# A causal mask moved from a TensorE product into the VectorE instruction that takes the row maximum

## The chip, the cores and the metric

The kernel runs on one core of a Trainium2 chip. The metric is the device time of one execution in microseconds (us), lower is better. Three executions of the kernel before took 1413.13 to 1418.58 us, with a median of 1417.94 us.

## The reference

One layer over a batch of 2 sequences with 1024 positions and 256 features: layer norm, causal attention with 16 heads of 128, a residual, layer norm, a mixture of 32 experts (8 chosen per token, group-limited) with two shared experts, and a residual. What the change touches is the masking and the row maximum of the softmax:

```python
scores = jnp.einsum('biph,biqh->biqp', k, q)
mask = jnp.tril(jnp.ones((pos, pos), dtype=x.dtype))
masked = scores * mask - jnp.float32(10000000000.0) * (1.0 - mask)
attn = jax.nn.softmax(masked / jnp.sqrt(jnp.float32(d_head)), axis=-1)
z = jnp.einsum('biqp,biph->biqh', attn, v)
```

All inputs are float32. The kernel keeps that accuracy by splitting each operand of a product into a high and a low part and adding three products (hi·hi, lo·hi, hi·lo), in the functions `three` and its callers.

## The kernel before

**Tiles and rows.** Queries are cut into 8 blocks of 128 per sequence. For one head and one block r (0 to 7), a "row" here means the 128 queries of that block against their first `width(r)` = 128(r+1) keys. There are 2 sequences × 16 heads × 8 blocks = 256 such rows. Heads are handled two at a time (a "pair", 16 in all), so a pair has 16 rows.

**The life of a row.** TensorE computes its scores into one of two PSUM tensors `ps_s` of 1024 columns (`scores`, line 820 onwards). VectorE takes the negated row maximum `neg_max` (`maximum`, line 1310). ScalarE computes exp(score + neg_max) into `prob` and sums it with its accumulator (`exponentials`, line 1113). Once all four rows of a half (`c` = 0 or 1, 512 queries) are done, TensorE transposes `prob` block by block (`transpose`, line 841), ScalarE and VectorE split each transposed block into `pT_hi` and `pT_lo` (lines 1132 and 1327), and TensorE multiplies by v (`times_v`) and by W_O (`project_out`). A PSUM tensor is free for the row after next when that row's exponential is done.

**The mask before.** Line 827 issues, ahead of a row's scores, one bf16 product of `ident_bf` (the weights) and `causal` (128 columns), a block that is 0 on and below the diagonal and -1e30 above. It starts the accumulation in the diagonal block, and the scores of the piece that holds this block are added to it. Scores are computed in pieces of up to 512 columns and at least 256. Row 4 (640 keys) therefore takes a piece of 512 and one of 256, 128 columns more than needed.

**The order.** Each engine follows the same order, written out by hand as a string of items per pair: `R` a row's scores, maximum and exponential, `T` a transposed block, `V` its product with v, `X` a projection for a later head, `W` the product with W_O. `PAIR` serves eleven plain pairs (the first seven and the twelfth to fifteenth); `MIDDLE`, `ROUTE`, `SLOTS`, `DISPATCH` and `LAST` add the layer norms, the routing of the experts and the first of their work:

```python
T0.0 R0.0 R0.1 T0.1 T0.2 X0 R0.2 R0.3 V0.0 T0.3 X1 V0.1 V0.2 T1.0 T1.1 V0.3 X2 R1.0 R1.1 W0.0
```

Items `R0.0` to `R0.3` are rows 4 to 7 of the pair's first head. `T1.0` needs all four of their exponentials. `R2.0` to `R2.3` and `T3.0` are the same for the second head. `SLOTS` and `DISPATCH` are `PAIR` with routing steps of VectorE woven in. After the last pair come the experts, with their weights loaded from DRAM.

Of the kernel before, what the change touches and what calls it, by code (L numbers as in the profile page):

```python
# [5 lines left out]
F32 = mybir.dt.float32  # L6
# [6 lines left out]
P = 128  # L13
# [266 lines left out]
def width(r):  # L280

    return P * (r + 1)


def layer(nc, x, w_a, w_b, w_o, router, bias, experts, out):
    with ExitStack() as ctx:
        build(nc, ctx, x, w_a, w_b, w_o, router, bias, experts, out)


def build(nc, ctx, x, w_a, w_b, w_o, router, bias, experts, out):  # L290
    def sb(name, shape, dt=F32, until=ctx):
        return until.enter_context(nc.sbuf_tensor(name, shape, dt))
# [11 lines left out]
    ident, ident_bf = sb("ident", [P, P]), sb("ident_bf", [P, P], BF16)  # L304
    causal = sb("causal", [P, P], BF16)
# [27 lines left out]
    number_int = sb("number_int", [1, TILES], mybir.dt.int32)[:, :]  # L333
# [9 lines left out]
    with ExitStack() as attention:  # L343
# [4 lines left out]
        raw = [sb(f"raw{n}", [P, GU + D], F32, attention) for n in range(2)]  # L348
# [75 lines left out]
    s_scores, s_max, s_exp = sem("scores"), sem("max"), sem("exp")  # L424
# [26 lines left out]
    CONSTS = 25 + WORD  # L451
# [123 lines left out]
    def _(pool):  # L575
# [3 lines left out]
        pool.memset(ident_bf[:, :], 0.0).then_inc(s_const, 1)  # L579
        pool.memset(causal[:, :], 0.0).then_inc(s_const, 1)  # L580
        pool.wait_ge(s_const, 5)
        for m in (ident, ident_bf):
            pool.affine_select(out=m[:, :], in_=m[:, :], compare_op=ALU.not_equal, fill=1.0,
                               base=0, pattern=[[-1, P]], channel_multiplier=1).then_inc(s_const, 1)
        pool.affine_select(out=causal[:, :], in_=causal[:, :], compare_op=ALU.is_ge, fill=MASKED,
# [61 lines left out]
        pool.wait_ge(s_const, 18 + 1 + WORD)  # L647
# [128 lines left out]
    def _(pe):  # L776
        pe.sem_inc(s_pv, PV0)
        pe.wait_ge(s_const, 8)

        def three(to, w_hi, w_lo, m_hi, m_lo, start, stop, joins=False):  # L780

            pe.matmul(to, w_hi, m_hi, start=start, stop=False, skip_group_check=joins)  # L782
            pe.matmul(to, w_hi, m_lo, start=False, stop=False, skip_group_check=joins)  # L783
            return pe.matmul(to, w_lo, m_hi, start=False, stop=stop, skip_group_check=joins)  # L784
# [35 lines left out]
        def scores(a, r, row, x_need):  # L820


            pe.wait_ge(s_exp, row + EXP0 - 1)
            pe.wait_ge(s_x_free, x_need + X0)
            q = slice(r * P, (r + 1) * P)
            to = ps_s[r % 2]
            pe.matmul(to[:, r * P:(r + 1) * P], ident_bf[:, :], causal[:, :], start=True, stop=False,
                      skip_group_check=True)
            for k0 in range(0, width(r), NQ):
                k1 = max(min(width(r), k0 + NQ), k0 + 2 * P)  # L830
                diagonal = k0 <= r * P < k1
                last = three(to[:, k0:k1], q_hi[a][:, q], q_lo[a][:, q], k_hi[a][:, k0:k1],
                             k_lo[a][:, k0:k1], not diagonal, True, diagonal)
            last.then_inc(s_scores, 1)
# [252 lines left out]
    def _(act):  # L1087
# [25 lines left out]
        def exponentials(r, row):  # L1113
            act.wait_ge(s_max, row + 1)
            c, j = r // BC, r % BC
            act.activation(prob[c][:, j, 0:width(r)], ps_s[r % 2][:, 0:width(r)], ACT.Exp,  # L1116
                           bias=neg_max[:, r:r + 1],
                           accum_out=row_sum[:, c, j:j + 1]).then_inc(s_exp, 1)
# [125 lines left out]
    def _(dve):  # L1244
# [65 lines left out]
        def maximum(r, row):  # L1310
            dve.wait_ge(s_scores, row + 1)
            dve.tensor_reduce(neg_max[:, r:r + 1], ps_s[r % 2][:, 0:width(r)], AX.X, ALU.max,  # L1312
                              negate=True).then_inc(s_max, 1)
# [351 lines left out]
```

## Time and profile before

| | |
|---|---|
| median of three executions | 1417.94 us |
| the three | 1417.94, 1418.58, 1413.13 us |
| span of the profiled execution, first to last instruction | 1405.0 us |
| the median less that span | 12.9 us |
| TensorE busy | 1328.9 us (95%) |
| TensorE weight loads | 1171.3 us (83%) |
| VectorE busy | 905.6 us (64%) |
| ScalarE busy | 722.3 us (51%) |
| GpSimd busy | 571.1 us (41%) |
| mean granted TensorE clock | 0.990 of full speed |

The profiled execution has no total of its own beside the three; its span is what stands in the rows, and what lies around it (launch, and the end after the last instruction) is the 12.9 us up to the median. In the rows, a time like "154.17 0.60" means start and duration in us, PE is TensorE's product, PEld its weight load, DVE is VectorE, ACT ScalarE, POOL GpSimd. The duration of one pipelined product overlaps that of the next; the pace at which products follow each other is read from their starts.

### The profile page before, as it was taken

Reading aid. Unit: us, or ns where it says so; the run is one execution under the profiler, and the core shown is the slowest. Engines: PE = TensorE matmul, PEld = TensorE weight load, DVE = VectorE, ACT = ScalarE, POOL = GpSimd, SP = SyncE. Lnnn points to the kernel's source line nnn. Section 1 sums busy time; section 2 is a strip of 40 time slices with the busy share of each in tenths; the row PEclk is TensorE's granted clock in tenths of the full one; section 3 lists DMA queues with packets and bytes.
Section 4 is the critical chain, followed back from the end, with each engine's and each line's share of the span. In section 5 each row is a group of like instructions: output and inputs, shape, how many; then the busy total and the mean of one; then the engine's idle time right before and its main releaser. Section 6 shows DMA issues by size and latency. Waiting matters only on the chain.

```text
span 1405.0 us, 28535 instructions
## 1 busy us (share of the span) xinstructions
PE 1328.9 (95%) x8578; PEld 1171.3 (83%) x8578; DVE 905.6 (64%) x1875; ACT 722.3 (51%) x1688; POOL 571.1 (41%) x587
## 2 busy tenths in 40 slices
PE   5999999999999899999999999999889997989998
PEld 4888888888888787888778888888779887978886
DVE  5667666666667878687886666666776632345536
ACT  2655555555555555554445555555455553545443
POOL 5535535355232223213043635441003664546554
PEclk9999999999999999999999999999999998999999
DMA  3253544525533000000001201020459996899963
GB/s 118 83 173 105 188 164 133 172 97 183 164 135 102 19 20 16 16 16 20 12 31 60 66 27 68 34 86 0 151 202 311 368 337 237 307 363 378 302 200 116
DMA packets 128246, 195.98 MB, mean 139 GB/s; under 512 B 10400, under 2 KB 99744, under 8 KB 128160
## 3 DMA queue, kind: packets, MB, share of 16 engines
q1 hardware_dynamic: 64752, 110.04, 23.4%
q10 hardware_dynamic: 51120, 51.26, 10.9%
q0 software_dynamic: 12288, 33.57, 6.8%
q8 instruction: 50, 0.82, 0.2%
q14 instruction: 36, 0.29, 0.1%
HBM read 107.79 MB, written 87.03 MB: 139 GB/s over the span
## 4 chain that ended last, share of the span: by engine, by line
PE 82%; DVE 7%; issue 3%; ACT 3%; DMA 3%; another core or an unknown queue 1%; SPq 1%; ACTq 0%; POOL 0%; POOLq 0%; DVEq 0%
PE ps_s L782 9%; PE ps_t L841 8%; PE ps_s L784 8%; PE ps_s L783 8%; PE ps_x L782 6%; PE ps_x L783 6%; PE ps_x L784 6%; PE ps_z L782 5%; PE ps_z L784 5%; PE ps_z L783 5%; PE ps_t L1006 3%; PE ps_z L1006 3%; PE ps_s L975 2%; PE ps_t L782 2%; PE ps_t L783 2%
## 5 line engine op out<-in xcount | busy, mean ns | idle before, releaser
L1116 ACT ACTIVATE prob<-ps_s,neg_max 128x128 f32<-128x128 f32 (+7 forms) x256 | 189.4, 741 | 256.3 <-DVE neg_max L1312 252.1
L1327 DVE TENSOR_TENSOR pT_lo<-ps_t,pT_hi 128x512 fp32r<-128x512 f32 (+2 forms) x320 | 189.4, 603 | 104.9 <-ACT pT_hi L1132 101.3
L1132 ACT ACTIVATE pT_hi<-ps_t 128x512 fp32r<-128x512 f32 (+2 forms) x320 | 161.4, 533 | 94.8 <-PE ps_t L841 92.1
L1312 DVE TENSOR_REDUCE neg_max<-ps_s 128x1 f32<-128x128 f32 (+7 forms) x256 | 186.8, 748 | 14.0 <-PE ps_s L784 11.5
L679 POOL DMA_INDIRECT xs<-xn,slots x128 | 127.7, 997 | 134.8 <-PE ps_z L1006 67.6
L841 PE MATMUL ps_t<-ident,prob 128*128 128x128 f32 x1152 | 170.8, 274 | 9.4 <-ACT prob L1116 4.2
L841 PEld LDWEIGHTS ps_t<-ident,prob 128*128 128x128 f32 x1152 | 136.7, 140 | 33.1 <-DVE pT_lo L1327 5.7
L782 PE MATMUL ps_s<-k_hi,q_hi 128*128 128x512 f32 (+2 forms) x384 | 154.7, 403 | 0.0
L1524 DVE TENSOR_TENSOR h<-sg,ps_s 128x256 f32<-128x256 f32 x112 | 46.9, 418 | 155.9 <-ACT sg L1166 103.9
L782 PE MATMUL ps_s<-ring,a_hi 128*128 x384 | 125.5, 327 | 14.3 <-SPq L530 11.9
L784 PE MATMUL ps_s<-k_hi,q_lo 128*128 128x512 f32 (+2 forms) x384 | 133.7, 348 | 0.0
L783 PE MATMUL ps_s<-k_lo,q_hi 128*128 128x512 f32 (+2 forms) x384 | 132.7, 346 | 0.0
L594 POOL TENSOR_TENSOR a_hi<-raw_a,zero 128x512 fp32r<-128x512 f32 x32 | 33.3, 1041 | 243.3 <-PE ps_x L784 158.3
L782 PE MATMUL ps_z<-pT_hi,v_hi 128*128 128x512 f32 (+2 forms) x320 | 121.8, 381 | 0.5 <-DVE pT_lo L1327 0.5
L784 PE MATMUL ps_z<-pT_hi,v_lo 128*128 128x512 f32 (+2 forms) x320 | 115.5, 361 | 0.0
L783 PE MATMUL ps_z<-pT_lo,v_hi 128*128 128x512 f32 (+2 forms) x320 | 115.4, 361 | 0.0
L1166 ACT ACTIVATE sg<-ps_s 128x256 f32<-128x256 f32 x112 | 43.5, 388 | 139.3 <-PE ps_s L784 82.2
L783 PE MATMUL ps_s<-ring,a_hi 128*128 x384 | 109.9, 286 | 0.1
L784 PE MATMUL ps_s<-ring,a_lo 128*128 x384 | 109.5, 285 | 0.0
L1342 DVE SCALAR_TENSOR_TENSOR acc<-ps_t,inv_sum,acc 128x256 f32<-128x256 f32 x256 | 108.2, 474 | 0.2 <-PE ps_t L784 0.2
L782 PEld LDWEIGHTS ps_s<-ring,a_hi 128*128 128x128 f32 x384 | 74.3, 194 | 24.3 <-issue 22.0
L594 POOL TENSOR_TENSOR o_hi<-raw_o,zero 128x256 fp32r<-128x256 f32 x32 | 20.7, 647 | 168.1 <-PE ps_z L784 167.8
(306 smaller groups left out, 3682.9 us busy)
## 6 DMA issues: line engine op xcount, KB each, us to landing
ring<-ws SPq DMA_DIRECT2D x56, 512.0 KB
xs<-taken SPq DMA_DIRECT2D x16, 1536.0 KB, 9.8
xq<-xs ACTq DMA_DIRECT2D x48, 512.0 KB
xs<-yq ACTq DMA_DIRECT2D x48, 512.0 KB
ws<-split_to SPq DMA_DIRECT2D x34, 512.0 KB, 3.1
raw<-experts_dram SPq DMA_DIRECT2D x34, 256.0 KB, 3.4
raw_a<-w_a_dram SPq DMA_DIRECT2D x15, 512.0 KB, 4.4
ring_down<-experts_dram SPq DMA_DIRECT2D x56, 128.0 KB
```

Of the source, the lines that this page charges most:

```text
L594: pool.tensor_tensor(hi, src, zero[:, 0:1].to_broadcast([P, src.shape[-1]]), ALU.add).then_inc(s_pool, 1)
L679: pool.indirect_dma_start(xs[b], bass.IndirectOffsetOnAxis(ap=slots[b][:, t, k:k + 1], axis=0), xn[:, t, :], None).then_inc(s_xs[b], 16)
L782: pe.matmul(to, w_hi, m_hi, start=start, stop=False, skip_group_check=joins)
L783: pe.matmul(to, w_hi, m_lo, start=False, stop=False, skip_group_check=joins)
L784: return pe.matmul(to, w_lo, m_hi, start=False, stop=stop, skip_group_check=joins)
L841: last = pe.transpose(bank[:, j * P:(j + 1) * P], prob[c][:, j, n * P:(n + 1) * P], ident[:, :])
L1006: last = pe.matmul(to, hT[g % 2][:, at], downs[g][j], start=what == "m" or j == 0, stop=what == "m" or j == 1)
L1116: act.activation(prob[c][:, j, 0:width(r)], ps_s[r % 2][:, 0:width(r)], ACT.Exp, bias=neg_max[:, r:r + 1], accum_out=row_sum[:, c, j:j + 1 ...
L1132: act.activation(to, ps_t[m % 2][:, j * P:], ACT.Copy).then_inc(s_hi, 1)
L1312: dve.tensor_reduce(neg_max[:, r:r + 1], ps_s[r % 2][:, 0:width(r)], AX.X, ALU.max, negate=True).then_inc(s_max, 1)
L1327: dve.tensor_tensor(lo, ps_t[m % 2][:, j * P:], hi.bitcast(F32), ALU.subtract).then_inc(s_bank_free, 1)
L1342: last = dve.scalar_tensor_tensor(to, ps_t[m % 2][:, j * D:(j + 1) * D], inv_sum[:, c, q:q + 1], to, ALU.mult, ALU.add)
```

## The change

The mask product and its identity go. `causal` becomes 128×1024, zero except for its last 128 columns, which hold the triangle, so that its last `width(r)` columns are the whole mask of row r. VectorE adds them in the instruction that takes the maximum. That instruction writes -(score + mask) back into PSUM and leaves the minimum of it in `neg_max`; ScalarE's exponential reads the negated scores with a scale of -1. Row 4 is put into columns 128 to 767 of its PSUM tensor and computed in pieces of 384 and 256 columns. A semaphore increment (`s_row`, for which nobody waits) stands between VectorE's wait and the new instruction. To make room, `raw[1]` shrinks to the part that is used, and `number_int` shares memory with `score`.

```diff
+def row_of(bank, r):
+    first = P if r == 4 else 0
+    return bank[:, first:first + max(width(r), 2 * P)]
...
-    ident, ident_bf = sb("ident", [P, P]), sb("ident_bf", [P, P], BF16)
-    causal = sb("causal", [P, P], BF16)
+    ident = sb("ident", [P, P])
+    causal = sb("causal", [P, S], BF16)
...
-    number_int = sb("number_int", [1, TILES], mybir.dt.int32)[:, :]
+    number_int = flat(score)[0:1, 0:TILES].bitcast(mybir.dt.int32)
...
-        raw = [sb(f"raw{n}", [P, GU + D], F32, attention) for n in range(2)]
+        raw = [sb(f"raw{n}", [P, GU + (D, 32)[n]], F32, attention) for n in range(2)]
...
-        pool.memset(ident_bf[:, :], 0.0).then_inc(s_const, 1)
         pool.memset(causal[:, :], 0.0).then_inc(s_const, 1)
-        pool.wait_ge(s_const, 5)
-        for m in (ident, ident_bf):
-            pool.affine_select(out=m[:, :], in_=m[:, :], compare_op=ALU.not_equal, fill=1.0,
-                               base=0, pattern=[[-1, P]], channel_multiplier=1).then_inc(s_const, 1)
-        pool.affine_select(out=causal[:, :], in_=causal[:, :], compare_op=ALU.is_ge, fill=MASKED,
+        pool.wait_ge(s_const, 4)
+        pool.affine_select(out=ident[:, :], in_=ident[:, :], compare_op=ALU.not_equal, fill=1.0,
+                           base=0, pattern=[[-1, P]], channel_multiplier=1).then_inc(s_const, 1)
+        pool.affine_select(out=causal[:, S - P:], in_=causal[:, S - P:], compare_op=ALU.is_ge, fill=MASKED,
                            base=0, pattern=[[-1, P]], channel_multiplier=1).then_inc(s_const, 1)
...
             q = slice(r * P, (r + 1) * P)
-            to = ps_s[r % 2]
-            pe.matmul(to[:, r * P:(r + 1) * P], ident_bf[:, :], causal[:, :], start=True, stop=False,
-                      skip_group_check=True)
-            for k0 in range(0, width(r), NQ):
-                k1 = max(min(width(r), k0 + NQ), k0 + 2 * P)
-                diagonal = k0 <= r * P < k1
+            to, k0 = row_of(ps_s[r % 2], r), 0
+            for k1 in [NQ - P, width(r)] if r == 4 else [NQ, width(r)] if r > 3 else [max(width(r), 2 * P)]:
                 last = three(to[:, k0:k1], q_hi[a][:, q], q_lo[a][:, q], k_hi[a][:, k0:k1],
-                             k_lo[a][:, k0:k1], not diagonal, True, diagonal)
+                             k_lo[a][:, k0:k1], True, True)
+                k0 = k1
             last.then_inc(s_scores, 1)
...
-            act.activation(prob[c][:, j, 0:width(r)], ps_s[r % 2][:, 0:width(r)], ACT.Exp,
-                           bias=neg_max[:, r:r + 1],
+            act.activation(prob[c][:, j, 0:width(r)], row_of(ps_s[r % 2], r)[:, 0:width(r)], ACT.Exp,
+                           bias=neg_max[:, r:r + 1], scale=-1.0,
                            accum_out=row_sum[:, c, j:j + 1]).then_inc(s_exp, 1)
...
             dve.wait_ge(s_scores, row + 1)
-            dve.tensor_reduce(neg_max[:, r:r + 1], ps_s[r % 2][:, 0:width(r)], AX.X, ALU.max,
-                              negate=True).then_inc(s_max, 1)
+            dve.sem_inc(s_row, 1)
+            row = row_of(ps_s[r % 2], r)[:, 0:width(r)]
+            dve.tensor_tensor_reduce(out=row, in0=row, in1=causal[:, S - width(r):], scale=-1.0,
+                                     scalar=-NEVER, op0=ALU.add, op1=ALU.min,
+                                     accum_out=neg_max[:, r:r + 1]).then_inc(s_max, 1)
```

The string that orders the items is the same; what changes is what an item issues. On TensorE, the start of a plain pair (`T0.0`, then the scores of rows 4 and 5) stood like this before; the rows name line, operation, output and inputs, and columns:

```order
L841 MATMUL ps_t<-ident,prob 128x128 x4
L823 REGISTER_ALU
L824 ISA
L827 MATMUL ps_s<-causal,ident_bf 128x128
L782 MATMUL ps_s<-k_hi,q_hi 128x512
L783 MATMUL ps_s<-k_lo,q_hi 128x512
L784 MATMUL ps_s<-k_hi,q_lo 128x512
L782 MATMUL ps_s<-k_hi,q_hi 128x256
L783 MATMUL ps_s<-k_lo,q_hi 128x256
L784 MATMUL ps_s<-k_hi,q_lo 128x256
L827 MATMUL ps_s<-causal,ident_bf 128x128
L782 MATMUL ps_s<-k_hi,q_hi 128x512
```

The same place in the changed kernel, where the lines of the three products are 787 to 789:

```order
L843 MATMUL ps_t<-ident,prob 128x128 x4
L828 REGISTER_ALU
L829 ISA
L787 MATMUL ps_s<-k_hi,q_hi 128x384
L788 MATMUL ps_s<-k_lo,q_hi 128x384
L789 MATMUL ps_s<-k_hi,q_lo 128x384
L787 MATMUL ps_s<-k_hi,q_hi 128x256
L788 MATMUL ps_s<-k_lo,q_hi 128x256
L789 MATMUL ps_s<-k_hi,q_lo 128x256
L787 MATMUL ps_s<-k_hi,q_hi 128x512
```

Both mask products are gone and row 4's first piece has 384 columns; nothing else moved. On VectorE, the same stretch before (`T0.0`'s low part, the reciprocal, the maxima of rows 4 and 5, and the next low part):

```order
L1327 TENSOR_TENSOR pT_lo<-ps_t,pT_hi 128x512
L1331 RECIPROCAL inv_sum<-row_sum 128x4
L1311 ISA
L1312 TENSOR_REDUCE neg_max<-ps_s 128x1
L1311 REGISTER_ALU
L1312 TENSOR_REDUCE neg_max<-ps_s 128x1
L1326 REGISTER_ALU
L1327 TENSOR_TENSOR pT_lo<-ps_t,pT_hi 128x384
```

and in the changed kernel:

```order
L1332 TENSOR_TENSOR pT_lo<-ps_t,pT_hi 128x512
L1336 RECIPROCAL inv_sum<-row_sum 128x4
L1313 ISA
L1316 ISA ps_s,neg_max<-ps_s,causal 128x640
L1316 ISA neg_max 128x1
L1313 REGISTER_ALU
L1316 ISA ps_s,neg_max<-ps_s,causal 128x768
L1316 ISA neg_max 128x1
L1331 REGISTER_ALU
L1332 TENSOR_TENSOR pT_lo<-ps_t,pT_hi 128x384
```

Each maximum has become two instructions: one that passes over the row, and one that only writes `neg_max`, 128x1.

## Rows read from the trace of the kernel before

**Rows 1.** The page: busy time of each engine, share of the span, instructions.

```profile
PE 1328.9 (95%) x8578; PEld 1171.3 (83%) x8578; DVE 905.6 (64%) x1875; ACT 722.3 (51%) x1688; POOL 571.1 (41%) x587
```

**Rows 2.** Stretches: start:end and length in us, then busy (instructions) of PE, PEld, DVE, ACT, POOL, granted clock, DMA share, GB/s.

```profile
156.25:215.21 58.96, 58.96 (x378) 51.95 (x377) 39.54 (x78) 32.55 (x76) 27.66 (x24) 1.00 0.46 151
...
650.69:718.57 67.88, 61.95 (x380) 52.34 (x379) 58.55 (x114) 32.51 (x78) 16.38 (x14) 1.00 0.05 16
sum 267.09, PE 251.69 PEld 215.78 DVE 213.33 ACT 135.51 POOL 64.76; mean PE 62.92 PEld 53.95 DVE 53.33 ACT 33.88 POOL 16.19
```

**Rows 3.** Order of time on PE in the third pair, from `T0.0` on.

```profile
154.17 0.60 PE L841 MATMUL ps_t<-ident,prob 128*128 128x128 f32 x4
154.61 0.22 PE L827 MATMUL ps_s<-causal,ident_bf 128*128 128x128 bf16 x1
...
154.95 0.39 PE L783 MATMUL ps_s<-k_lo,q_hi 128*128 128x512 f32 x1
155.18 0.40 PE L784 MATMUL ps_s<-k_hi,q_lo 128*128 128x512 f32 x1
...
155.77 0.23 PE L827 MATMUL ps_s<-causal,ident_bf 128*128 128x128 bf16 x1
...
156.12 0.39 PE L783 MATMUL ps_s<-k_lo,q_hi 128*128 128x512 f32 x1
...
156.94 0.71 PE L841 MATMUL ps_t<-ident,prob 128*128 128x128 f32 x5
157.40 0.47 PE L782 MATMUL ps_x<-xT_hi,b_hi 128*128 128x512 f32 x1
157.71 0.39 PE L783 MATMUL ps_x<-xT_lo,b_hi 128*128 128x512 f32 x1
...
159.88 0.34 PE L783 MATMUL ps_s<-k_lo,q_hi 128*128 128x384 f32 x1
160.05 0.34 PE L784 MATMUL ps_s<-k_hi,q_lo 128*128 128x384 f32 x1
```

**Rows 4.** Groups by shape on DVE: count, busy us, mean ns, idle before.

```profile
L1312 DVE TENSOR_REDUCE neg_max<-ps_s 128x1 f32<-128x1024 f32 x32 | 39.1, 1221 | 4.9 <-PE ps_s L784 4.9
L1312 DVE TENSOR_REDUCE neg_max<-ps_s 128x1 f32<-128x896 f32 x32 | 34.6, 1080 | 0.4 <-PE ps_s L784 0.4
...
L1477 DVE TENSOR_TENSOR room<-room,best 128x1024 f32<-128x1024 f32 x2 | 2.4, 1215 | 0.0
```

**Rows 5.** The same view, one source more and one operation more: 256 columns from PSUM.

```profile
L1342 DVE SCALAR_TENSOR_TENSOR acc<-ps_t,inv_sum,acc 128x256 f32<-128x256 f32 x256 | 108.2, 474 | 0.2 <-PE ps_t L784 0.2
...
L1327 DVE TENSOR_TENSOR pT_lo<-ps_t,pT_hi 128x256 fp32r<-128x256 f32 x64 | 26.8, 418 | 16.0 <-ACT pT_hi L1132 14.7
```

**Rows 6.** Order of time on DVE in the same pair.

```profile
156.16 0.17 DVE L1331 RECIPROCAL inv_sum<-row_sum 128x4 f32<-128x4 f32 x1
156.25 1.85 DVE L1312 TENSOR_REDUCE neg_max<-ps_s 128x1 f32<-128x640 f32 x2
...
160.94 2.22 DVE L1312 TENSOR_REDUCE neg_max<-ps_s 128x1 f32<-128x896 f32 x2
```

**Rows 7.** Order of time on ACT and PEld: row 7's exponential and `T1.0`.

```profile
163.20 1.12 ACT L1116 ACTIVATE prob<-ps_s,neg_max 128x1024 f32<-128x1024 f32 x1
164.21 0.19 ACT L1116 ACTIVATION_READ_ACCUMULATOR prob<-ps_s,neg_max 128x1 f32 x1
...
164.72 0.57 PEld L841 LDWEIGHTS ps_t<-ident,prob 128*128 128x128 f32 x5
```

**Rows 8.** The second head of the same pair, ACT and PE: row 7, `T3.0`.

```profile
192.91 0.19 ACT L1116 ACTIVATION_READ_ACCUMULATOR prob<-ps_s,neg_max 128x1 f32 x1
...
194.23 1.03 PE L841 MATMUL ps_t<-ident,prob 128*128 128x128 f32 x8
```

**Rows 9.** Stretch around a fall of the granted clock (columns as in rows 2).

```profile
478.00:484.00 6.00, 4.20 (x21) 3.67 (x22) 5.00 (x9) 2.88 (x6) 2.87 (x3) 0.61 0.22 70
```

**Rows 10.** Order of time on POOL at the start, its first wait.

```profile
8.68 1.05 POOL L603 TENSOR_TENSOR inv<-var,neg_half 128x4 f32<-128x4 f32 x1 [6.29 <-DVE var L1263]
```

More of the change, by code:

```diff
@@ L423, in build @@
     s_pool = sem("pool_hi")
-    s_scores, s_max, s_exp = sem("scores"), sem("max"), sem("exp")
+    s_scores, s_row, s_max, s_exp = sem("scores"), sem("row"), sem("max"), sem("exp")
     s_bank, s_hi, s_bank_free = sem("bank"), sem("pT_hi"), sem("bank_free")
@@ L450, in build @@
     WS0, YS0 = 16, 16
-    CONSTS = 25 + WORD
+    CONSTS = 23 + WORD
     X_SCORES = [X0 + x_before + count_of(order, ("M", b, 0)) + 1
@@ L646, in _ @@
         pool.iota(thr_int, pattern=[[P, NT]], base=0, channel_multiplier=0).then_inc(s_const, 1)
-        pool.wait_ge(s_const, 18 + 1 + WORD)
+        pool.wait_ge(s_const, 16 + 1 + WORD)
         pool.tensor_copy(number[:, :], number_int).then_inc(s_const, 1)
@@ L777, in _, with three @@
         pe.sem_inc(s_pv, PV0)
[L778 to L784, printed above, removed]
+        pe.wait_ge(s_const, 6)
+        def three(to, w_hi, w_lo, m_hi, m_lo, start, stop):
+            pe.matmul(to, w_hi, m_hi, start=start, stop=False)
+            pe.matmul(to, w_hi, m_lo, start=False, stop=False)
+            return pe.matmul(to, w_lo, m_hi, start=False, stop=stop)
         def transpose_xn(q, d, bank):
```

## The prediction

> **What bounds the kernel now.** I read the page's busy times first [rows 1]: TensorE is busy for 95% of the span, VectorE for 64%, ScalarE for 51%. The average hides stages, so the second view was the stretch of one pair from row 4 to the next pair's row 4 [rows 2]. In a plain pair TensorE is busy for all of its 58.96 us, VectorE for 39.5, ScalarE for 32.6: TensorE sets the pace, and whatever leaves its queue is time won as long as the other engines keep up. In the four pairs with layer norm and routing in them (`MIDDLE` to `DISPATCH`, together 267.1 us) TensorE is busy for 251.7 us and VectorE for 213.3, and in the last of them for 61.95 and 58.55 of 67.88 us: there TensorE waits for VectorE in places. The third view is the order of time [rows 3, 6, 7], which tells what a mask product costs and how close the other engines are behind.
>
> **Removed: 256 mask products.** A product's cost is its part of the pace. Before row 5, the mask starts at 155.77 and the second score product at 156.12, 0.35 us for the mask and the first score product [rows 3]. The next 512-column product takes 0.23 (154.95 to 155.18). So the mask costs 0.12 us: a few hundredths of its own, and the rest in the product behind it, whose weights had no long product to load under. Behind transposes one could think that the following product is late anyway. Four transposes, mask and first product take 0.78 us (154.17 to 154.95), five transposes and a first product without a mask 0.77 (156.94 to 157.71), so one transpose (about 0.11) pays for the mask there too, and 0.12 us stands. 256 × 0.12 = **30.7 us**.
>
> **Removed: 128 columns of row 4.** Three products of 512 + 256 columns become three of 384 + 256. A product of 512 takes 0.23 us, one of 384 takes 0.17 to 0.18 (159.88 to 160.05), so 3 × 0.055 = 0.165 us per row 4, of which there are 32: **5.3 us**. TensorE's part is 36.0 us, and of a plain pair 16 × 0.12 + 2 × 0.165 = 2.25 us.
>
> **Changed: 256 maxima on VectorE.** The pass over the row is one source and one output more. For 1024 columns the reduction from PSUM takes 1221 ns and a two-source addition in SBUF, written in place, 1215 [rows 4], so another stream costs nothing that these rows show. None shows VectorE writing PSUM. New beyond doubt is the second instruction that only writes `neg_max`, and the increment of `s_row`. Lower bound for the addition per row: 0 (it hides, or the pass is as much shorter). Upper bound: ScalarE's instruction of the same kind takes 0.19 us [rows 7], and an operation more costs 474 - 418 = 56 ns in the pair of rows nearest to it [rows 5], together 0.25 us. The nearest row to a tiny VectorE instruction is the reciprocal of 128x4: it starts at 156.16 and the next at 156.25 [rows 6], 0.09 us. I take **0.12 us**, this and 0.03 for the increment and a longer start; 0 and 0.25 go to the range.
>
> **What covers this, and where the cover ends.** VectorE has 19 us free in a plain pair and 16 × 0.12 = 1.9 us more is no load. The delay counts where TensorE waits for an exponential. The tightest place is `T1.0`: row 7's sum is out at 164.21 + 0.19 = 164.40 and the weight load of `T1.0` starts at 164.72, a margin of 0.32 us [rows 7]. The path to it is one chain through all four maxima of the head (rows 4 and 5 back to back from 156.25, rows 6 and 7 from 160.94 [rows 6], their exponentials, and low parts between), which starts behind the projection ahead of `T0.0`. Between `T0.0` and `T1.0` TensorE itself loses four masks and one row 4, 0.645 us, so it would come 0.33 us before row 7 is ready, even if the maxima cost what they did; four maxima at 0.12 add 0.48. `T1.0` then waits for 0.81 us. A plain pair keeps 2.25 - 0.81 = 1.44 us. The second head's place is wider: its sum is out at 193.10 and `T3.0` starts at 194.23 [rows 8], 1.13 us against 0.645 + 0.48, just enough. Eleven plain pairs: **15.8 us**.
>
> In the four full pairs, in which TensorE is idle for 15.4 us already [rows 2], I take the margin of 0.32 us as used up, and of the twelve other maxima I count half on the path, 0.72 us: 2.25 - 0.81 - 0.32 - 0.72 = 0.4 us, four times: **2 us** rounded. `LAST` has 12 rows, two of them row 4: 1.77 - 0.81 = **1 us**. The first four rows, ahead of the pairs: **0.5 us**.
>
> **Costed at nothing.** GpSimd's longer memset of `causal` (its time at the start is covered by a wait of 6.29 us [rows 10]; if it were not, less than 1 us), the shared memory, the smaller `raw[1]`, and ScalarE's scale. The experts come behind and move as a block; their waits for weight loads start from the end of attention.
>
> **Sum.** 15.8 + 2 + 1 + 0.5 = 19.3 us. Span 1405.0 - 19.3 = 1385.7; the 12.9 us around it up to the median give 1398.6, say **1399 us**, 1.3% under the median of 1417.94.
>
> **Rivals.**
> *A. The maxima cost no more, and little is given back.* For it: the equal rows of 1221 and 1215 ns. Against it: two instructions stand where one did. At 0 us per row a plain pair keeps 2.25 - 0.33 = 1.92, eleven keep 21, the full four 1.6 each, the rest 2.5: 30 us, 1388. Chance 0.15.
> *B. The maxima cost 0.25 us.* `T1.0` waits 0.33 + 1.0, a plain pair keeps 0.92, eleven keep 10. In the full pairs 2.25 - 1.33 - 0.32 - 1.5 = -0.9 each, `LAST` and the first rows give 0.9: 8 us, 1410. Chance 0.17, and 0.08 beside it that the full pairs lose more still, so that nothing is seen (1411 to 1425).
> *C. Slower: the pass runs at half pace, because it reads and writes the same PSUM bank.* No row here has VectorE write PSUM, so nothing excludes it. 128 columns cost 1221 - 1080 = 141 ns [rows 4]. Rows 4 to 7 have 26 such blocks, 3.7 us more in the chain to `T1.0`, which then waits 4.5 us. The chain to `T3.0` gets the same, and with its margin and idle stretches I count 1.9. A plain pair would lose 4.5 + 1.9 - 2.25 = 4.15, eleven 46; the full pairs would get 10 us of VectorE work on top of 53 and lose 8 each: 32. That is 1496 us. It decides from a mean of (2.25 - 0.33) / 4 = 0.48 us more per maximum of rows 4 to 7, where a plain pair gains nothing. Chance 0.09.
> [...]
> *D. Slower through the clock.* [...] Against it: the pair from 650.69 has 5.9 us of idle TensorE in it and a clock of 1.00 [rows 2]. Chance 0.03.
>
> **The numbers.** The forecast has 0.48, A 0.15, B 0.25 with its tail, C and D 0.12. Faster by over 0.5% (under 1410.8; about 0.5% is what a measurement of this kernel can tell from no change): the forecast, A, and most of B's 0.17, 0.77. Within 0.5%: 0.11. Slower: 0.12. The range runs from 1386, just under A, to 1414, just over B; outside it are C, D and part of B's tail.
>
> **What would show it.** No mask products: 8322 products on TensorE instead of 8578, as the pieces keep their number. The start-to-start pace of a plain pair 57.5 us instead of 58.96, with TensorE waiting for the exponential at `T1.0` by about 0.8 us and nowhere else. The new pass at 1.22 us for 1024 columns, the instruction behind it at 0.09 us of pace. Wrong would be: a pass of over 2 us for 1024 columns (C), waits of the full pairs over 5 us more than before (B's tail), a lower clock within the pairs (D), or no wait at `T1.0` (A).

## The result and the profile after

| | before | after |
|---|---|---|
| median, us | 1416.13 (4 executions, 1413.13 to 1418.58) | 1396.44 (4 executions, 1393.97 to 1397.29) |
| ratio after / before, 95% interval | | 0.9866, 0.9846 to 0.9886 |
| span of the profiled execution | 1405.0 | 1394.4 |

The change makes the kernel 1.3% faster, as forecast (1399 us). The page of the changed kernel, busy times of the engines, against [rows 1]:

```profile
PE 1302.5 (93%) x8322; PEld 1155.3 (83%) x8322; DVE 915.7 (66%) x2131; ACT 720.8 (52%) x1688; POOL 571.7 (41%) x585
```

TensorE has 256 products and 26.4 us of work less, VectorE 256 instructions and 10.1 us more. The same stretches as in [rows 2], from a pair's row 4 to the next pair's: a plain pair, then the last of the four full ones.

```profile
153.04:210.47 57.43, 57.23 (x362) 50.91 (x361) 40.12 (x94) 32.55 (x76) 27.66 (x24) 1.00 0.46 156
...
637.69:705.86 68.17, 59.98 (x364) 51.19 (x363) 59.11 (x131) 32.64 (x78) 16.82 (x15) 1.00 0.05 16
```

The plain pair went from 58.96 to 57.43 us. TensorE is now idle for 0.2 us in it, which it never was before. The full pair, 67.88 before, is 0.3 us longer: VectorE is busy for 59.11 us of it, 58.55 before, and TensorE is idle for 8.2 us instead of 5.9; its waits for an exponential grew from 1.7 to 2.9 us.

**VectorE's new instructions**, groups by shape in the columns of [rows 4]:

```profile
L1316 DVE CUSTOM_DVE_ANT_0 ps_s<-ps_s,causal 128x1024 f32<-128x1024 f32 x32 | 40.1, 1252 | 0.0
L1316 DVE DVE_READ_ACCUMULATOR2_ANT neg_max<- 128x1 f32 x256 | 36.1, 141 | 0.0
L1316 DVE CUSTOM_DVE_ANT_0 ps_s<-ps_s,causal 128x896 f32<-128x896 f32 x32 | 34.9, 1091 | 0.2 <-PE ps_s L789 0.2
```

A pass that reads PSUM and `causal` and writes PSUM takes 1252 ns for 1024 columns where the reduction took 1221, and 1091 for 896 where it took 1080. The second source, the second operation and the writing back into PSUM together cost 31 and 11 ns. So with one source in PSUM, the other the bf16 `causal`, and the output in PSUM, the pass isn't at half pace: rival C needed over 2 us for 1024 columns.

In order of time on DVE, the chain to `T1.0` in the third pair (start, duration), beside [rows 6]:

```profile
153.04 0.81 DVE L1316 CUSTOM_DVE_ANT_0 ps_s<-ps_s,causal 128x640 f32<-128x640 f32 x1
153.76 0.14 DVE L1316 DVE_READ_ACCUMULATOR2_ANT neg_max<- 128x1 f32 x1
153.76 1.00 DVE L1316 CUSTOM_DVE_ANT_0 ps_s<-ps_s,causal 128x768 f32<-128x768 f32 x1
...
158.67 1.26 DVE L1316 CUSTOM_DVE_ANT_0 ps_s<-ps_s,causal 128x1024 f32<-128x1024 f32 x1
159.85 0.14 DVE L1316 DVE_READ_ACCUMULATOR2_ANT neg_max<- 128x1 f32 x1
```

The instruction that writes `neg_max` and the next pass start at the same moment, 153.76. It costs VectorE no pace here; but ScalarE can only start when it is over (159.85 + 0.14 = 159.99, and the exponential stands at 160.02 below).

And its end on ACT, then on PE, beside [rows 7]:

```profile
160.02 1.11 ACT L1118 ACTIVATE prob<-ps_s,neg_max 128x1024 f32<-128x1024 f32 x1
161.04 0.19 ACT L1118 ACTIVATION_READ_ACCUMULATOR prob<-ps_s,neg_max 128x1 f32 x1
```

```profile
160.69 0.28 PE L788 MATMUL ps_z<-pT_lo,v_hi 128*128 128x256 f32 x1
160.81 0.28 PE L789 MATMUL ps_z<-pT_hi,v_lo 128*128 128x256 f32 x1
161.28 1.15 PE L843 MATMUL ps_t<-ident,prob 128*128 128x128 f32 x8 [0.20 <-ACT prob L1118]
162.19 0.36 PE L787 MATMUL ps_z<-pL_hi,v_hi 128*128 128x256 f32 x1
```

Row 7's sum is out at 161.23 and `T1.0` starts at 161.28: a margin of 0.05 where it was 0.42 to the product and 0.32 to its weight load. The products before it go at 0.12 us, so `T1.0` would have started at 160.93 and waits for 0.35 us. This is the wait that the prediction named, at less than half of its length. The second head's margin shrank from 1.13 to 0.90 us and decides nothing.

### The profile page after: what moved, and what is told of

Its sections match the earlier page's. It is cut to its first block, busy times and chain, and to the rows that moved or that the text cites. A ratio compares the mean times of both kernels' runs of the same rounds, so it can differ in the third digit from the quotient of the medians.

```text
span 1394.4 us, 28532 instructions
## 1 busy us (share of the span) xinstructions
PE 1302.5 (93%) x8322; PEld 1155.3 (83%) x8322; DVE 915.7 (66%) x2131; ACT 720.8 (52%) x1688; POOL 571.7 (41%) x585
## 4 chain that ended last, share of the span: by engine, by line
PE 67%; DVE 12%; issue 9%; ACT 5%; DMA 3%; another core or an unknown queue 2%; SPq 1%; ACTq 1%; DVEq 0%; POOL 0%; POOLq 0%
PE ps_t L843 7%; PE ps_s L787 6%; PE ps_s L789 6%; PE ps_s L788 6%; PE ps_x L787 5%; PE ps_x L788 5%; PE ps_x L789 5%; PE ps_z L787 4%; PE ps_z L789 4%; PE ps_z L788 4%; DVE ps_s L1316 4%; DMA ring_down<-experts_dram 3%; PE ps_z L1008 3%; PE ps_t L1008 3%
## 5 line engine op out<-in xcount | busy, mean ns | idle before, releaser
L1316 DVE CUSTOM_DVE_ANT_0 ps_s<-ps_s,causal 128x128 f32<-128x128 f32 (+7 forms) x256 | 190.3, 769 | 5.7 <-remote 3.5
L843 PE MATMUL ps_t<-ident,prob 128*128 128x128 f32 x1152 | 172.2, 275 | 17.0 <-ACT prob L1118 10.6
L787 PE MATMUL ps_s<-k_hi,q_hi 128*128 128x512 f32 (+2 forms) x384 | 141.3, 368 | 1.2 <-DVE k_lo L1309 1.1
```

What stands on the lines that cost most here:

```text
L787: pe.matmul(to, w_hi, m_hi, start=start, stop=False)
L843: last = pe.transpose(bank[:, j * P:(j + 1) * P], prob[c][:, j, n * P:(n + 1) * P], ident[:, :])
L1316: dve.tensor_tensor_reduce(out=row, in0=row, in1=causal[:, S - width(r):], scale=-1.0, scalar=-NEVER, op0=ALU.add, op1=ALU.min, accum_out= ...
```

## The experiments

The runs stood on four chips of one kind, here A to D, and each ratio is to the kernel before on the same chip: 1408.7 us on A, 1414.6 on B, 1377.0 on C and 1414.8 on D. A pair's time is always from its row 4 to the next pair's, from the profiled execution.

### Row 4 alone, masks kept (A)

```diff
-            for k0 in range(0, width(r), NQ):
-                k1 = max(min(width(r), k0 + NQ), k0 + 2 * P)
+            for k1 in [NQ - P, width(r)] if r == 4 else ...
```

> The kernel before with one part of the change alone: row 4 in columns 128 to 767, in pieces of 384 and 256. Theory (TensorE pays for every column and there is margin at T1.0): 3 x 0.055 = 0.165 us per row 4, a plain pair of the first seven 58.63 us instead of 58.96, 4 to 5 us in all. Rival (the first-row weights or a wait eat it, so that the pieces give nothing): 58.96 us and no difference.

Measured: 1403.84 us (9 executions), ratio 0.9974 (0.9957 to 0.9991). A plain pair takes 58.63, 0.33 less, as worked out in the prediction. Item by item of TensorE's order (start to start), `R0.0` got 0.153 and `R2.0` 0.162 us shorter, and no other item moved by more than 0.02.

### Masks left out, nothing else (A)

```diff
-            pe.matmul(to[:, r * P:(r + 1) * P], ident_bf[:, :], causal[:, :], start=True, stop=False,
-                      skip_group_check=True)
```

This kernel leaves the causal mask out of the computation.

> The kernel before without the mask products and without any mask; the causal mask is left out of the computation, maxima as before, pieces of 512 and 256. Theory: 16 x 0.12 us less of TensorE per pair, of which T1.0 gives back 0.48 - 0.32 = 0.16, so 57.2 us per plain pair of the first seven. If pairs 12 to 15 were paced by something other than TensorE's queue, as in the changed kernel, they stay at 59.8 us and the whole is 16 to 19 us faster; if that was due to VectorE's new instructions, they fall to 58.0 and the whole is 24 us faster.

Measured: 1384.68 us (4), ratio 0.9827 (0.9803 to 0.9851), 24 us faster. Pairs 12 to 14 take 57.80, 57.83 and 57.82 us, which is the number of the branch that blamed VectorE's new instructions. The cause it named can't be right, as the kernel before has 59.8 us there without them; the scatters below give another, and the 24 us aren't the price of the masks alone.

A plain pair takes 57.41, almost what it takes in the changed kernel, though row 4 still has its 768 columns. The expected 57.2 had a wait at `T1.0` in it. There is none: the margin is 0.14 us. The chain from the start of row 4's pass to row 7's sum takes 7.95 us here and 8.15 before, because row 5's scores come earlier too. Before, row 5's pass waited for them and started 0.89 us behind row 4's (156.25 in [rows 6]):

```profile
157.14 0.96 DVE L1312 TENSOR_REDUCE neg_max<-ps_s 128x1 f32<-128x768 f32 x1
```

Here it starts 0.71 us behind, right after row 4's, and in the changed kernel 0.72 (153.04 and 153.76 above). In a plain pair of the changed kernel, then, the 0.33 us of row 4 and what the passes on VectorE cost cancel.

Item by item the masks are worth 0.10 to 0.14 us in each of the 16 rows, behind transposes too, 1.83 in sum. Of it 0.27 comes back where no mask stood: `T1.1`, `V0.3` and `X2` (0.17), `V3.6` (0.09). These are hand-overs of their own. In the second to sixth pair, `T1.1` starts 0.06 to 0.08 us behind the end of VectorE's `pL_lo`, which frees its PSUM tensor, where it was 0.36 before; `X2` 0.05 behind `k_lo`, which frees `ps_x`, where it was 0.27; and `V3.6` 0.05 behind `pT_lo`, its input, where it was 0.15 to 0.17. TensorE comes so early there that it meets the other engine's work, with no wait long enough to stand in the list of waits.

### The changed kernel with a product of the mask's shape put back (A)

```diff
             to, k0 = row_of(ps_s[r % 2], r), 0
+            pe.matmul(to[:, r * P:(r + 1) * P], causal[:, S - P:], causal[:, 0:P], start=True, stop=True)
```

> The changed kernel with a product of the mask's shape put back in front of each row (128 columns, bf16, own weights), whose result the scores overwrite. Theory: TensorE's queue is back but for row 4, and VectorE's new instructions are covered: a plain pair of the first seven 58.65 us, the whole 4 us faster than before and 15 us slower than the changed kernel. Rival (a good part of the gain came from VectorE or from elsewhere, such as the chip that ran it): the whole stays near the changed kernel's time. Rival (the new instructions cost on their own, more than 0.1 us per row): 59.3 us or more and slower than before.

Measured: 1410.87 us (10), ratio 1.0015 (1.0002 to 1.0028). The whole gain is gone, so it came from the products. The sizes were missed: the whole was expected 4 us faster than before and is 2 us slower, and a plain pair takes 58.87, not 58.65. Against the kernel with row 4 alone VectorE's new form costs 7.0 us. In the two profiles 1.5 us of that lie in the first seven plain pairs and 3.0 in the four full pairs (268.36 and 265.37 us), 1.8 of them in the first, which varies by 1.0 us between executions of the changed kernel; the rest lies in pairs 12 to 15, whose pace varies too. In a plain pair it is 0.24 us more than with row 4 alone. That kernel differs by VectorE's passes and by what its extra product reads and how the scores join it. The items say where:

| item | row 4 alone | product put back | |
|---|---|---|---|
| `T1.0` | 0.437 | 0.479 | +0.042 |
| `T1.1` | 0.356 | 0.412 | +0.056 |
| `V0.3` | 0.437 | 0.471 | +0.034 |
| `X2` | 1.390 | 1.505 | +0.115 |

No other item differs by over 0.02. TensorE doesn't wait for anything here (its pace into `T1.0` is 0.118 us, the margin 0.07), and still the four items from `T1.0` on take 0.25 us more. With a margin of 0.42 they don't. Here too `T1.1` starts 0.05 us behind `pL_lo` (0.36 with row 4 alone) and `X2` 0.05 behind `k_lo` (0.26). Both of these values are made behind row 7's exponential and come later with it.

The chain from row 4's pass to row 7's sum is 0.34 us longer than in the other kernel, 8.33 against 8.00: here VectorE's new form costs **0.085 us per maximum**. About 0.1 us of the 0.34 belong to this kernel: row 5's pass, whose scores have only just arrived, starts 0.89 us behind row 4's, where the reduction started 0.74 behind. In the changed kernel the pass starts 0.72 behind, and its chain of 8.19 us against the 7.95 without masks, where no pass waits for scores either, gives **0.06 us per maximum**. The passes of 640 to 1024 columns are 0.01 to 0.04 us longer than the reductions, 0.023 in the mean. The rest is the write of `neg_max`, which delays ScalarE by 0.06 to 0.07 us behind rows 5 and 7; the increment of `s_row` is in it and wasn't priced alone.

### Row 4 back to 512 + 256 in the changed kernel (B)

```diff
-            for k1 in [NQ - P, width(r)] if r == 4 else ...
+            for k1 in [NQ, NQ + 2 * P] if r == 4 else ...
```

`row_of` starts row 4 at column 0 again.

> The changed kernel with row 4 in pieces of 512 and 256 as before. Theory (what TensorE saves ahead of T1.0 is taken by the wait there, the second head's row 4 stays won): 57.43 + 0.17 = 57.6 us per plain pair. If T1.0's wait took nothing of it: 57.76 us. If it took all: 57.43 us. Whole kernel 2 to 3 us slower than the changed one.

Measured: 1398.02 us (4), ratio 0.9896 (0.9872 to 0.9919), 2.9 us above the changed kernel on the same chip. A plain pair takes 57.66, 0.23 more. `R0.0` and `R2.0` lose 0.175 each, and `V0.2`, the item in which TensorE waits for `T1.0`, gets 0.110 shorter. Row 4's narrower piece in the first head is thus worth only a third of its size; the second head's is kept in full.

### The scatters of the experts' rows left out (A)

The changed kernel's plain pairs take 57.43 us, but the stretches of pairs 12 to 14, by the same string, took 59.84, 59.80 and 59.79, and before the change 59.87, 59.75 and 59.76. What these pairs have beside the others are GpSimd's scatters, 16 per pair. This kernel leaves the 64 scatters out, so the experts of the first sequence compute on zeros:

```diff
                 pool.wait_ge(s_pv, PV0 + p * TRS + v)
-                scatter(0, (p - PAIRS - 3) * 16 + done + n)
+                pool.sem_inc(s_xs[0], 16)
```

> The changed kernel, with GpSimd's 64 scatters of the first sequence's tokens in pairs 12 to 15 left out (a semaphore increment stands for each, so the experts of the first sequence compute on zeros). Theory (GpSimd's bursts of indirect DMAs hold back TensorE's semaphore increments by about 1.5 us, so that T2.0 waits and pairs 12 to 15 keep 59.8 us): those pairs fall to 57.4 us, 8 to 9 us in all. Rival (the pace comes from the code of those pairs, their loop or their instruction loads, not from the DMAs): 59.8 us as before.

Measured: 1384.62 us (4), ratio 0.9832 (0.9812 to 0.9853). Pairs 12 to 14 take 57.44, 57.49 and 57.42: plain pairs again. Pair 15 takes 56.56, and the four together 228.91 us, 7.7 to 8.5 less than in three executions of the changed kernel with the scatters; 8 to 9 were expected. What the scatters do is seen in two places of pair 12 of the changed kernel (chip D). The first, on DVE, then on PE:

```profile
729.23 0.28 DVE L1332 TENSOR_TENSOR pL_lo<-ps_t,pL_hi 128x128 fp32r<-128x128 f32 x1
731.15 0.70 DVE L1316 CUSTOM_DVE_ANT_0 ps_s<-ps_s,causal 128x512 f32<-128x512 f32 x1 [1.64 <-remote]
```

```profile
728.76 0.39 PE L789 MATMUL ps_s<-k_hi,q_lo 128*128 128x512 f32 x1
...
732.77 0.98 PE L843 MATMUL ps_t<-ident,prob 128*128 128x128 f32 x7 [1.00 <-ACT prob L1118]
```

The last product of `R1.3` ends at 729.15, but VectorE, idle since 729.51, gets to its row only at 731.15, 2.0 us behind. In plain pairs the lag is 0.27. Row 3's exponential is late by that much, and TensorE stands at `T2.0` for 1.0 us: the 1.7 us of extra lag less the margin of 0.64 that `T2.0` has in plain pairs. The second place is the projection `X8`, on ACT, then on PE:

```profile
748.72 0.38 ACT L1106 ACTIVATE v_raw<-ps_x 128x256 f32<-128x256 f32 x1 [2.17 <-remote]
```

```profile
746.79 0.28 PE L789 MATMUL ps_x<-a_hi,xT_lo 128*128 128x256 f32 x1
...
749.89 0.39 PE L787 MATMUL ps_x<-a_hi,xT_hi 128*128 128x256 f32 x1 [0.96 <-DVE v_lo L1300]
```

`X8`'s last product ends at 747.07 and ScalarE gets to it at 748.72, 1.65 us behind; in plain pairs the lag is 0.04. VectorE's `v_lo` is late with it, and TensorE stands at `X9` for 1.0 us. Start to start, the two places take 1.2 us each of the 2.4 by which the pair is longer than a plain one. Without the scatters both lags are gone (0.27 and 0.04 us).

### The changed kernel again (B)

> The changed kernel unaltered, for a comparison on the chip of the other experiments. Plain pairs 57.43 us, pairs 12 to 14 59.8 us; ratio to the kernel before 0.987 as on the first chip, so 1390 us where the kernel before takes 1408.

Measured: 1395.1 us (4), ratio 0.9874 (0.985 to 0.9898). Plain pairs 57.43, pairs 12 to 14 59.81, 59.85 and 58.75. In the third, `R1.3`'s pass starts 23.18 us behind row 4's, as in plain pairs, and 24.9 in the two others. Of the 1.3 us by which the third is longer than plain, 1.1 stand at `X9`, as ScalarE starts 1.52 us behind `X8`.

### Scatters placed otherwise (B)

The changed kernel issues 3, 8 and 5 scatters per pair, at three places of GpSimd's order. These kernels issue 3, 2 and 11, and 3, 4 and 9. The diff is that of the first; the second has `(5, 7, 9, 11)` and `range(14, 23), 7`.

```diff
-                paced_scatters(p, range(5, 13), 3)
+                paced_scatters(p, range(5, 7), 3)
...
-                paced_scatters(p, range(14, 19), 11)
+                paced_scatters(p, range(14, 25), 5)
```

> The changed kernel with GpSimd's scatters of pairs 12 to 15 at other places: 3, 2 and 11 per pair instead of 3, 8 and 5, so that none runs in the microseconds ahead of the scores of row 3 of the second head (R1.3). Theory (a burst of indirect DMAs holds back TensorE's increments, and R1.3 is where this hurts): pairs 12 to 14 fall to about 57.5 us, 6 to 7 us in all. Rival (the late burst holds back other increments with less slack, the transposes of T3): 58.5 us or more, little gained.

> The same scatters, 3, 4 and 9 per pair, each behind another product with v, so that few stand back to back. Theory that it takes a burst: 57.5 to 58 us in pairs 12 to 14. Rival (each single scatter holds increments back): 59 us or more.

Measured: 1400.07 us, ratio 0.9901 (0.9877 to 0.9924), and 1398.47 us, ratio 0.9884 (0.9865 to 0.9903). `R1.3`'s lag is gone in both (its pass starts 23.2 us behind row 4's as in plain pairs), and pairs 12 to 14 still take 59.7 and 59.5. The wait for `v_lo` stays (3.7 and 3.6 us in 4 waits; 2.9 in 4 in the changed kernel on this chip), and one for `z_lo` is new (2.6 and 2.5 us in 4), behind an exchange whose lag was 0.3 us before and is 1.4 us here. So the delay went with the scatters that were moved, and the one at `X8` remained. Both expected gains stayed out, and neither kernel beats the changed one.

### V0.3 ahead of T1.0, and X2 ahead of T1.0 (C)

Two attempts to put work under the wait at `T1.0`, by the string of the plain pair alone:

```diff
-... V0.2 T1.0 T1.1 V0.3 X2 R1.0 ...
+... V0.2 V0.3 T1.0 T1.1 X2 R1.0 ...
```

```diff
-... V0.2 T1.0 T1.1 V0.3 X2 R1.0 ...
+... V0.2 X2 T1.0 T1.1 V0.3 R1.0 ...
```

> The changed kernel with one item of the plain pair moved on all engines: V0.3 stands ahead of T1.0 instead of behind T1.1. If the wait of TensorE at T1.0 (0.35 us, and a slower restart of about 0.1) is what eats the gain of row 4 there, V0.3's three products (about 0.36 us) lie under it: a plain pair takes 57.0 to 57.1 instead of 57.43, 13 pairs by this string give 4 to 5 us, the kernel takes about 1391. Rival: the wait is only moved, to the scores of row 0 of the other half or to X2, and the pair stays at 57.43, the kernel at 1396. Slower: the split of T0.3 isn't ready so early and V0.3 waits for it.

> The changed kernel with X2 ahead of T1.0 instead of behind V0.3. X2 is over 1 us of products, more than T1.0's wait, so TensorE would not wait there at all: a plain pair 57.0 if nothing else is late. Rival: T1.0 and T1.1 come later by what is left of X2 and the low parts that follow them make V1.0 or R1.0 wait, or X2 itself waits for its bank, since X1 stands closer before it: a plain pair of 57.4 or more, the kernel at 1396 or above.

Measured: 1362.12 us (4), ratio 0.9892 (0.9877 to 0.9907), and 1398.73 us (5), ratio 1.0154 (1.014 to 1.0167). Both fail: a plain pair takes 57.75 and 60.24. PE in the first, then PE in the second, each at its new wait:

```profile
161.85 0.28 PE L789 MATMUL ps_z<-pT_hi,v_lo 128*128 128x256 f32 x1
162.82 0.39 PE L787 MATMUL ps_z<-pL_hi,v_hi 128*128 128x256 f32 x1 [0.68 <-DVE pL_lo L1332]
163.04 0.28 PE L788 MATMUL ps_z<-pL_lo,v_hi 128*128 128x256 f32 x1
```

```profile
169.29 0.50 PE L787 MATMUL ps_x<-xT_hi,b_hi 128*128 128x512 f32 x1 [1.58 <-DVE k_lo L1309]
```

`V0.3` needs `pL_lo`, whose high part ScalarE makes only behind row 7's exponential (161.13 in the changed kernel), later than `T1.0` could start. `X2`, right behind `V0.2`, finds X1 still in `ps_x`: it waits 1.58 us for VectorE's `k_lo` (161.92 in the changed kernel), which stands behind row 7's pass and ScalarE's `k_hi`. Neither leaves room under the wait. The changed kernel itself didn't run on C, so the ratios can't be set against its own; the pace of a plain pair, 57.43 in three executions on other chips, can.

In one point both runs differ from those of the changed kernel on B: pairs 12 to 14 take 57.79, 57.74 and 57.79 in the first and 60.25, 60.23 and 60.25 in the second, each kernel's plain pace, with all their scatters in them. `R1.3`'s row there, DVE then PE:

```profile
730.21 0.69 DVE L1316 CUSTOM_DVE_ANT_0 ps_s<-ps_s,causal 128x512 f32<-128x512 f32 x1
```

```profile
729.54 0.40 PE L789 MATMUL ps_s<-k_hi,q_lo 128*128 128x512 f32 x1
```

The product ends at 729.94 and the pass starts 0.27 us behind it, though GpSimd issues a scatter every 1.27 us here as well. At `X8` the lag is 0.04 us.

### Both kernels on one chip (D)

> The kernel before, once more, for a profile on the same chip as the changed kernel's. In the runs so far with the scatters in them pairs 12 to 14 took 59.5 to 60.7 us, but in the two last runs (V0.3 first, X2 first), on a chip where the kernel before took 1377 us, they took what the plain pairs take. If the late increments are a property of the chip and not of the kernel, then where the kernel before has a median of about 1377, its pairs 12 to 14 take 58.96 like the plain ones and what follows the last pair about 423 us; where it has about 1416, they take 59.8 and 448.

> The changed kernel once more, on the same chip as the run before it. Plain pairs 57.43 on any chip. If the chip is one where the kernel before takes about 1377, pairs 12 to 14 take 57.4 too, attention gains 11 x 1.52 + 1.9 + 1 = 20 us or a little more between the spans, and the ratio comes near 0.985. If it is one of about 1416, pairs 12 to 14 stay at 59.8 and the ratio at 0.987 has to come from somewhere behind the pairs.

Measured: the kernel before 1415.07 us (12 executions), ratio 0.9997 (0.9983 to 1.0011); the changed kernel 1396.27 us (5), ratio 0.9884 (0.9865 to 0.9903). The profiled execution of the kernel before took 1415.76 us around a span of 1414.0. Its stretches (columns as in [rows 2]), the four full pairs, pairs 12 to 14, pair 15, and what follows:

```profile
451.88:719.03 267.15, 251.71 (x1559) 215.81 (x1558) 213.36 (x460) 135.57 (x317) 64.76 (x70) 0.99 0.06 17
719.03:901.19 182.16, 178.32 (x1130) 156.14 (x1129) 118.87 (x230) 96.69 (x228) 86.54 (x84) 1.00 0.16 52
901.19:961.08 59.89, 58.74 (x373) 51.34 (x372) 38.95 (x76) 31.76 (x75) 27.58 (x27) 1.00 0.17 59
961.08:1414.00 452.92, 405.62 (x2770) 365.12 (x2768) 237.00 (x529) 217.78 (x509) 195.67 (x198) 0.98 0.74 254
```

The same stretches of the changed kernel, in an execution of 1396.27 us around a span of 1394.5:

```profile
441.77:706.24 264.47, 244.08 (x1495) 211.24 (x1495) 215.39 (x525) 135.17 (x317) 65.16 (x71) 0.99 0.06 17
706.24:884.94 178.70, 173.34 (x1082) 153.08 (x1081) 120.72 (x278) 96.72 (x228) 86.35 (x83) 1.00 0.16 53
884.94:942.99 58.05, 56.97 (x358) 50.29 (x357) 39.59 (x92) 31.80 (x75) 27.57 (x27) 1.00 0.18 61
942.99:1394.50 451.51, 404.68 (x2758) 363.56 (x2755) 237.33 (x542) 217.76 (x509) 197.00 (x198) 0.98 0.74 255
```

| stretch | forecast gain | gain, us |
|---|---|---|
| up to the first pair's row 4 | 0.5 | -0.43 |
| first seven plain pairs | 7 x 1.44 = 10.1 | 10.56 (413.11 to 402.55) |
| four full pairs | 2 | 2.68 |
| pairs 12 to 14 | 4.3 | 3.46 |
| pair 15 | 1.4 | 1.84 |
| last pair and experts | 1 | 1.41 |
| sum of the span | 19.3 | 19.5 |

The first and last rows are no gain or loss of the change. The first row 4 starts at 37.6 to 39.4 us in all these profiles, in no order. The last pair itself, from its row 4 to its last product with W_O, takes 53.22 us before and 53.31 after, and the experts behind it take 394.8 to 399.7 us in five executions of these two kernels.

In this execution of the kernel before pairs 12 to 14 took 60.9, 60.7 and 60.6 us, 1 us more each than in the profile ahead of the prediction, and 59.8 was expected on such a chip. The extra us is the wait at `X9`: ScalarE gets to `X8` 1.6 us behind it here and 0.8 us in the first profile, where the 0.78 us of margin in a plain pair just covered that. The changed kernel's first profile had the 1.6 us, and a wait at `T2.0` longer by 0.5 us, so between the two first profiles these pairs kept nothing. The pair of executions whose spans, 1405.0 and 1394.4, differ by 10.6 us misled: the first was a quick one, in these pairs and in the experts (448 us against 453). The changed kernel's pairs 12 to 14 take 59.86, 59.93 and 58.91 us here, about the expected 59.8, but its gain doesn't come from behind the pairs, as was expected with that: nearly all of it lies in them.

## Why the prediction was right, point by point

**Removed: the mask products, 0.12 us each, 30.7 us.** Right as a price in the plain pairs. Their items in a plain pair sum to 1.83 us in the kernel without masks and to 1.90 in the changed one, against 16 x 0.12 = 1.92. That transposes ahead of them hide nothing is right too.

**Removed: 128 columns of row 4, 0.165 us each.** Right: 0.153 and 0.162 where it was done alone.

**Changed: the maxima, 0.12 us each.** Right in kind, too large: 0.06 us on the chain of the changed kernel, 0.085 where a pass waits for its scores. The reasoning about the small instruction took its pace from the reciprocal [rows 6], 0.09 us; in fact it has none (153.76 and 153.76), and what counts is that ScalarE starts 0.06 to 0.07 us later behind it, on two of the chain's four rows, and 0.023 us of a longer pass.

**`T1.0` waits 0.81 us.** The place was right and the length wrong: it waits 0.35 us. The prediction let TensorE come 0.645 us earlier and row 7's sum 0.48 us later, and took 0.32 us of margin off. TensorE does come 0.65 us earlier. The margin is 0.42 us to the product, of which a hand-over with a wait keeps 0.05. But the sum comes only 0.06 us later behind `T0.0`: the new form adds 0.24 us to the chain, and earlier scores for row 5 take 0.19 off it, which the prediction left out. That gives 0.65 - 0.37 + 0.06 = 0.34 us. Against this, 0.25 us is lost in the three items behind `T1.0` and in `T1.0` itself, and 0.11 in `V3.6`. No step named these: they are the hand-overs at `T1.1`, `X2` and `V3.6`, none of which had more than 0.36 us of margin. The plain pair's balance is 1.90 + 0.32 - 0.34 - 0.25 - 0.11 = 1.52 us kept, against 1.44. That it came out so close is luck: a wait forecast 0.46 us too long stands against 0.36 us of losses that weren't forecast.

**`T3.0`, just enough.** It held, with 0.90 us to spare where the prediction had nearly nothing. Leaving the masks out alone keeps this margin at 1.13 us: in the second head VectorE's chain waits for TensorE's scores and comes earlier with them, so TensorE's saving doesn't count against it. Only the new form's 0.23 us do.

**Full pairs 2 us, `LAST` 1 us, first rows 0.5 us.** The full pairs gave 1.9 us in the profile after and 2.7 on chip D. The size holds, but 0.4 us for each of the four was an average of unequal ones: +1.35, +0.74, +0.10 and -0.29 us. In the last, where VectorE was busiest, the change costs time, as rival B had it: it takes 67.56 us with the masks left out and the old reductions, and 68.17 in the changed kernel. `LAST` gave nothing (53.22 and 53.31 us), and for the first rows no gain shows above the variation. These 1.5 us of the forecast were wrong; on chip D the first rows lost 0.43 us and what follows the last pair gained 1.41 by variation.

**Eleven plain pairs, 15.8 us.** Here a step was wrong and its sum right. Four of the eleven aren't plain: scatters run in them, and in three the pace is set by late hand-overs at `R1.3` and `X8`, 59.8 us in place of 58.96. The trace ahead of the prediction showed it in their paces, and I read one plain pair for eleven. Those three kept nothing between the two first profiles and 3.46 us between the two on chip D, where all eleven kept 10.56 + 5.30 = 15.9. That this sum meets the forecast is luck too: it depends on which executions are set side by side.

**The 12.9 us around the span.** Wrong: 1.8 us lie around it (1415.76 and 1414.0; 1396.21 and 1394.4). The other 11 were an execution quicker than the three that were timed. The gain was taken off the median in the end, so the forecast didn't depend on it.

**The rivals.** A (the maxima free) fell by 0.085 us and the wait at `T1.0`. B had the right place with three to four times the price. C fell with the 1252 ns for 1024 columns. D (the clock of [rows 9] in every pair) fell: the clock is 1.00 in the plain pairs, with a wait of 0.35 us in each.

## What to carry to other kernels

Here, work that left the bounding engine was won in full only up to the margins of the hand-overs behind it: 2.2 us per pair were taken from TensorE and 0.7 went to four hand-overs, 0.35 to the one with the wait, and as much to three whose margins had been 0.36, 0.27 and 0.15 us. So list every margin shorter than what is taken away ahead of it, not the tightest alone, and ask of each producer whether its own inputs come earlier too. Read the pace of each repetition in a trace, not of one for all; and compare two profiles only stretch by stretch, with a second execution of each, before a difference of under 1% is believed.

## What the runs showed of the hardware

**At `T1.0`, `T1.1` and `X2` the hand-overs cost more than their wait.** With a margin of 0.07 us and no wait at all at `T1.0`, it and the three items behind took 0.25 us more than with 0.42. TensorE no longer runs ahead of its products with its weight loads there. In the changed kernel, PEld at `T1.0` and `X2`, then VectorE's `k_lo`, which frees the PSUM tensor of `X2`:

```profile
160.69 0.19 PEld L789 LDWEIGHTS ps_z<-pT_hi,v_lo 128*128 128x128 f32 x1
161.28 0.92 PEld L843 LDWEIGHTS ps_t<-ident,prob 128*128 128x128 f32 x8 [0.40 <-ACT prob L1118]
...
162.66 0.19 PEld L787 LDWEIGHTS ps_x<-xT_hi,b_hi 128*128 128x128 f32 x1
```

```profile
161.92 0.69 DVE L1309 TENSOR_TENSOR k_lo<-ps_x,k_hi 128x512 fp32r<-128x512 f32 x1 [0.20 <-ACT k_hi L1112]
```

The load of `T1.0` starts with its product, at 161.28, where before it started 0.10 us ahead of it, under the last product of `V0.2` (164.72 [rows 7] and 164.82). That of `X2` starts 0.05 us behind the end of `k_lo` at 162.61, with the product at 162.67; before it stood 0.12 us ahead of its product (165.93 and 166.05). In the kernel with the product put back the first product of `X2` then takes 0.34 us to the next one, where it took 0.23. So the loss sits at three hand-overs, `T1.0`, `T1.1` and `X2`. That the weight load makes it longer than the lateness is an inference from these starts; nothing was run that separates it.

**The accumulator's read took nothing of VectorE's pace in 167 of 256 places.** Each takes 141 ns, and those 167 start in the same 0.02 us as the instruction behind them. With the product put back, row 5's pass, whose scores had only just come, started 0.03 us behind the read's end instead.

**With the scatters other engines' hand-overs came later, on A, B and D.** With GpSimd's indirect DMAs running, VectorE started 1.5 to 2.0 us behind the end of TensorE's product at `R1.3`, and ScalarE 0.8 to 1.6 us behind `X8`, pair after pair, in both first profiles and on chips A, B and D. At `X8` each of pairs 12 to 14 had it there, at `R1.3` not every one. Leaving the scatters out, on A, brought the lags to 0.27 and 0.04 us; moving them, on B, removed the one at `R1.3`, left the one at `X8` and made a new one of 1.4 us ahead of `z_lo`. In the kernel without masks, on A, `R1.3` had no extra lag and `X8` had 0.8 us. Both runs on C had none at either place with all scatters in them. There the kernel before takes 1377 us instead of 1409 to 1415, and what follows the row 4 of the last pair takes 423 and 425 us instead of 448 to 456. Every kernel with scatters in it that ran elsewhere showed a lag, which points to the chip; but neither kernel that ran on C ran elsewhere, so whether it is the chip or the moment at which a scatter falls stays open. So does what makes it: no run took the scatters apart.

**Not tried:** the increment of `s_row`. A kernel without it, which would price it alone, wasn't run, so the 0.06 and 0.085 us contain it.
